# q and k stored as stacked rows, maxima passed through DRAM: a decoder layer in float32 on one core

## The chip, the cores and the metric

The kernel runs on one core of a Trainium2 chip. The metric is the device time of one execution in microseconds, median of three runs. Engines are named as in the profile: PE (TensorE matmul) and PEld (its weight load), DVE (VectorE), ACT (ScalarE), POOL (GpSimd), SP (SyncE). SP computes nothing: it issues nearly all DMAs and waits on semaphores between them.

## The reference

Input x is [8, 256, 256] in float32, 2048 tokens of width 256. Three blocks are applied in turn, each to a layer norm of x and added to x:

1. a gated state-space mixer (projections, a depthwise convolution, a cumulative product and sum along the sequence);
2. attention. The reference passes the normed x as queries and a second tensor as keys and values: `q = Q @ WQ + bQ`, `k = K @ WK + bK`, `v = V @ WV + bV`, 16 heads of 16 columns each, `scores = q k^T / 4` with a causal mask over 256 x 256, a softmax, the product with v, and `@ WO + bO`;
3. a mixture of 8 experts, the top 2 of each token with a capacity per expert.

## The kernel before

The program has two functions that run one after the other with a barrier between their blocks.

**The first, mixer_and_projections**, runs the mixer over four blocks of 512 tokens and computes q, k and v. q and k are kept in two float32r parts, high and low (the low part is the value less its high part), in the tiles `qkh` and `qkl` of [128 features, 2, 512 tokens]. The same two tiles serve k of one block and q of another in turn, so ACT's `k_high` and `q_high` wait until the stores of the other have landed. `store` (L265) writes each part to its own DRAM tensor, `qd[0]`, `qd[1]`, `kd[0]`, `kd[1]`, with one DMA of 128 partitions each. Before the block ends SP waits for all stores.

**The second, attention_route_experts**, goes over 16 groups g. A group is one sequence b of 256 tokens and one half k of the heads (8 heads: 4 pairs, the two heads of a pair at partitions 0 and 64). Each group has three steps s, so there are 48 steps. A step of a group does, by engine:

- PE `scores(u)` (L1363): a first product of q and k, used only for the row maxima of the softmax. DVE `maxima(u)` (L1574) reduces it to one number per query and head.
- PE `turn_maxima(g)` (L1424), once in a group: turns the maxima of the three steps into rows. ACT `maxima_high` and DVE `maxima_low` (L1578) split them into two parts in the tile `mt` of [8 heads, 2 parts, 256].
- SP `maxima(g)` (L1091): copies these rows into the tile `q3` of the group, under the rows of q, one DMA of 1 KB per head and part (16 DMAs a group).
- PE `turned(n)` (L1389): the product again, the other way round, over 50 rows: 16 rows of q high, 16 of q high, 16 of q low against k high, k low, k high (a product in two parts each), and two rows of maxima against rows of -1, so that the maximum is subtracted in the product. It waits for `m_in`, the landing of the maxima.
- ACT `exps(n)` (L1243), PE `weigh(n)` (L1411) against v and against ones, DVE `divide(g)` (L1583, L1586).

The order of each engine is written out by hand, over a step counter t. PE runs `scores(t + LEAD)` beside `turned(t)`, with LEAD = 6, `turn_maxima(g)` in step t = 3g - 3 and `weigh(t - 1)`; masks are added to each product first (L1350, L1375), which wait for DVE's maxima and for ACT's exponentials of the step before, since each product has one PSUM buffer of two banks. Routing of a block of 512 tokens is strewn in between at fixed offsets in the steps: PROJECT, BOTH, NORM, TURN, LOGITS (DVE `choose`, L1610 to L1632), RANKS (`place`, L1638 to L1646) and SEND (POOL `scatter`, L1173). After the last step come the rest of the routing and the experts, which PE bounds (L101, L1516).

SP's list in this function is: `lay(0)`, `lay(1)`, values and small weights, `lay(2)`, `values(1)`, the first expert's weights (two DMAs of 1 MB), `lay(3)`, and then for each g: `lay(g + 2)`, `maxima(g)`, sometimes `values` and `store_base`. `lay(g)` (L1082) fills `q3` and `k3` of a group, 48 rows for each of the two heads of a pair, with 12 DMAs of 64 KB onto 16 partitions each; there are 4 such pairs of tiles (ITEMS), and `lay(g)` waits until `turned` of group g - 4 is done. The first `lay` waits for eight memsets of POOL (L1204) that write the rows of -1.

Of the kernel before, what the change touches and what calls it, by code (L numbers as in the profile page):

```python
# [14 lines left out]
P = 128  # L15
# [153 lines left out]
def mixer_and_projections(nc, sems, c, x_sb, bo, a, disp, qd, kd, vd):  # L169

    with ExitStack() as ctx:
# [69 lines left out]
        with nc.Block() as block:  # L241

            @block.sync
            def _(sp):
# [64 lines left out]
                sp.wait_ge(S["q_st"], 32 * NBLK)  # L309
                sp.wait_ge(S["k_st"], 32 * NBLK)  # L310
# [73 lines left out]
            def _(act):  # L384
# [93 lines left out]
                def k_high(i):  # L478
                    if i == 0:
                        act.wait_ge(S["in_rest"], 80)  # L480
                    for m in range(DC):
                        act.wait_ge(S["k"], DC * i + m + 1)
                        ge(act, S["k_st"], 32 * i)
                        ge(act, S["q_st"], 32 * (i - 1))
# [8 lines left out]
                def q_high(i):  # L493
                    for m in range(DC):
                        act.wait_ge(S["q"], DC * i + m + 1)
                        act.wait_ge(S["k_st"], 32 * upto(i + 2))
                        ge(act, S["q_st"], 32 * i)
# [487 lines left out]
def attention_route_experts(nc, sems, c, x_sb, bo, wo_w, router_w, qd, kd, vd, disp, w1, w2, out):  # L985
# [9 lines left out]
    LEAD = 6  # L995
    ITEMS = 4
    LAID = 16 * 12
    PROJECT, BOTH, NORM, TURN, LOGITS, RANKS, SEND = 8, 14, 16, 17, 20, 23, 24
    END = 12 * (NBLK - 1) + SEND + TPB * K

    with ExitStack() as ctx:
# [68 lines left out]
        with nc.Block(no_gpsimd_drain=True) as block:  # L1070

            @block.sync
            def _(sp):
                def lay(g):
                    b, k = divmod(g, 2)
                    ge(sp, A["st"], 3 * (g - ITEMS + 1))
                    for m, srcs in ((q3[g % ITEMS], (qd[0], qd[0], qd[1])), (k3[g % ITEMS], (kd[0], kd[1], kd[0]))):
                        for n, src in enumerate(srcs):
                            heads = src[k * P:(k + 1) * P, b * L:(b + 1) * L].rearrange("(p e r) t -> e r p t", p=4, e=2)
                            for e in range(2):  # L1080
                                at = 64 * e + HD * n
# [51 lines left out]
                for g in range(GR):  # L1133
# [105 lines left out]
            def _(act):  # L1239
# [5 lines left out]
                def maxima_high(g):  # L1245
                    act.wait_ge(A["mT"], g + 1)
                    ge(act, A[f"m_in{g % 2}"], 256 * (g // 2))
# [51 lines left out]
                maxima_high(0)  # L1299
                for t in range(END):  # L1300
                    if t < NS:
                        exps(t)
                    if t % 3 == 0 and t // 3 + 1 < GR:
                        maxima_high(t // 3 + 1)
# [32 lines left out]
            def _(pe):  # L1337
# [40 lines left out]
                def turned(n):  # L1378
                    g, s = divmod(n, 3)
                    if s == 0:  # L1380
                        pe.wait_ge(A[f"m_in{g % 2}"], 256 * (g // 2 + 1))
# [34 lines left out]
                def turn_maxima(g):  # L1416
                    pe.wait_ge(A["nm"], 3 * g + 3)
                    ge(pe, A["ml"], g)
                    i = (3 * g - 3 - LOGITS) // 12
                    ge(pe, R["i8"], TPB * (i + 1))  # L1420
                    i = (3 * g - 3 - RANKS) // 12
# [33 lines left out]
                def logits(i):  # L1455
                    pe.wait_ge(S["xt"], 2 * (i + 1))
                    pe.wait_ge(A["ml"], min(4 * i + 8, GR))
# [8 lines left out]
                def ranks(i):  # L1466
                    pe.wait_ge(R["both"], i + 1)
                    pe.wait_ge(A["ml"], min(4 * i + 9, GR))
# [321 lines left out]
```

## Time and profile before

| | |
|---|---|
| median of 3 runs | 905.03 us (902.49 to 905.58) |
| the profiled execution's own time | 904.72 us |
| its span, first to last instruction | 903.0 us |
| first function, up to the stores' landing | 0 to about 271 us |
| attention: head, up to the first `turned` | about 271 to 320 us |
| attention: `turned` of 16 groups | 320 to 572 us |
| rest of the routing | 572 to 616 us |
| experts and their output | 616 to 903 us |
| PE busy | 678.1 us (75%) |
| DVE, ACT, POOL busy | 56%, 38%, 36% |

The busy shares are means over stages with different limits. The chain that ended last is followed back from the last instruction; "SPq" in it is time in which SP's queue was issuing DMAs one after another.

### The profile page before, as it was taken

To read this page: it belongs to the slowest core of one execution; us is meant where nothing else is said; L and a number is where in the kernel's file an instruction comes from. 1 tells how busy PE (TensorE), PEld (TensorE's weight loads), DVE (VectorE), ACT (ScalarE), POOL (GpSimd) and SP (SyncE) were. 2 spreads that over 40 slices of the span, in tenths; PEclk is the share of its full clock that TensorE was granted. 3 is DMA by queue.
4 is the path that set the end of the run, shared out by engine and by line. 5 is a ranking of instruction groups with operands and counts; after the bars stand their busy time and mean duration, and the time that the engine had idled before them with its cause. 6 is when DMAs were issued, how large, how long until landed. Compare 5 with 4: busy or idle time off the path is not lost.

```text
span 903.0 us, 13776 instructions
## 1 busy us (share of the span) xinstructions
PE 678.1 (75%) x4984; PEld 561.2 (62%) x4984; DVE 508.2 (56%) x985; ACT 346.5 (38%) x674; POOL 325.3 (36%) x307
## 2 busy tenths in 40 slices
PE   3869989798642357667667857733999999999992
PEld 2548877687431134344344535423999999999992
DVE  6686877869431224444544533422678777787741
ACT  4555647244310022223223213112556556565541
POOL 1326232423007000001113013052457776866855
PEclk9889999999875566879977878755999999999997
DMA  9002056211213632222323311115043454351213
GB/s 293 16 25 94 24 189 211 97 48 52 88 46 95 198 109 57 60 75 57 92 53 112 89 50 58 31 32 186 1 130 62 107 144 96 75 144 17 31 20 40
DMA packets 65987, 76.81 MB, mean 85 GB/s; under 512 B 17739, under 2 KB 52566, under 8 KB 65920
## 3 DMA queue, kind: packets, MB, share of 16 engines
q1 hardware_dynamic: 56704, 68.12, 23.8%
q0 software_dynamic: 9216, 7.81, 6.1%
q8 instruction: 40, 0.66, 0.3%
q14 instruction: 27, 0.22, 0.1%
HBM read 47.75 MB, written 29.64 MB: 86 GB/s over the span
## 4 chain that ended last, share of the span: by engine, by line
SPq 28%; PE 28%; issue 6%; POOL 4%; DMA 2%; DVE 1%; ACT 1%; POOLq 0%
SPq L1091 17%; PE w_bank L1516 13%; PE w_bank L101 11%; SPq L1082 10%; POOL out L1197 2%; PE w_bank L1485 1%; DMA a_q<-a_mt 1%; POOL a_k L1204 1%; POOL disp L1173 1%; POOL w_hl L1186 1%; DMA w_rows<-disp 1%; PE a_turned L1389 0%; DMA out<-w_y,w_to 0%; PE a_out L1411 0%; PE a_shared L1462 0%
## 5 line engine op out<-in xcount | busy, mean ns | idle before, releaser
L1574 DVE TENSOR_REDUCE a_nm<-a_scores 128x4 f32<-128x1024 f32 (+1 forms) x48 | 58.6, 1221 | 158.4 <-PE a_scores L1363 158.4
L1243 ACT ACTIVATE a_pr<-a_turned 128x1024 f32<-128x1024 f32 x48 | 49.2, 1025 | 197.5 <-PE a_turned L1389 197.5
L1516 PE MATMUL w_bank<-w_w2h,w_hh 128*108 128x256 f32 x384 | 108.6, 283 | 1.3 <-POOL w_hl L1186 1.3
L1516 PE MATMUL w_bank<-w_w2h,w_hl 128*108 128x256 f32 x384 | 107.8, 281 | 0.0
L1516 PE MATMUL w_bank<-w_w2l,w_hh 128*108 128x256 f32 x384 | 107.5, 280 | 0.0
L1677 DVE SCALAR_TENSOR_TENSOR w_v<-w_th,w_bank 128x324 f32<-128x324 f32 x128 | 62.8, 492 | 70.2 <-ACT w_th L1281 68.4
L1180 POOL TENSOR_TENSOR w_w1l<-w_s,w_w1h 128x256 fp32r<-128x256 f32 x64 | 56.7, 886 | 120.1 <-ACT w_w1h L1270 120.1
L1281 ACT ACTIVATE w_th<-w_bank 128x324 f32<-128x324 f32 x128 | 56.6, 443 | 99.8 <-PE w_bank L101 98.0
L1389 PE MATMUL a_turned<-a_q,a_k 50*128 50x256 f32 (+1 forms) x256 | 33.2, 364 | 81.9 <-DMA a_q<-a_mt 81.9
L1186 POOL TENSOR_TENSOR w_hl<-w_v,w_hh 128x324 fp32r<-128x324 f32 x64 | 56.5, 882 | 91.4 <-ACT w_hh L1287 91.4
L1389 PEld LDWEIGHTS a_turned<-a_q,a_k 50*128 50x128 f32 x256 | 22.3, 228 | 99.4 <-DMA a_q<-a_mt 90.2
L101 PE MATMUL w_bank<-w_xh,w_w1h 128*128 128x324 f32 x256 | 80.5, 315 | 1.1 <-ACT w_xh L1276 1.1
L101 PE MATMUL w_bank<-w_xh,w_w1l 128*128 128x324 f32 x256 | 80.1, 313 | 0.0
L1197 POOL DMA_INDIRECT out<-w_y,w_to x48 | 75.4, 1570 | 13.2 <-issue 9.9
L101 PE MATMUL w_bank<-w_xl,w_w1h 128*128 128x324 f32 x256 | 80.1, 313 | 0.0
L1653 DVE TENSOR_TENSOR w_w2l<-w_s,w_w2h 128x256 fp32r<-128x256 f32 x64 | 66.2, 1035 | 2.2
L1516 PEld LDWEIGHTS w_bank<-w_w2h,w_hh 128*108 128x108 f32 x384 | 65.8, 171 | 1.8 <-issue 1.8
L1516 PEld LDWEIGHTS w_bank<-w_w2l,w_hh 128*108 128x108 f32 x384 | 66.0, 172 | 0.0
L1516 PEld LDWEIGHTS w_bank<-w_w2h,w_hl 128*108 128x108 f32 x384 | 65.9, 172 | 0.0
L1287 ACT ACTIVATE w_hh<-w_v 128x324 fp32r<-128x324 f32 x128 | 60.3, 472 | 12.0 <-DVE w_v L1677 11.0
L101 PE MATMUL m_bank<-m_sh,m_wh 128*128 128x512 f32 x112 | 46.6, 416 | 10.3 <-ACT m_sh L422 6.9
L1173 POOL DMA_INDIRECT disp<-w_x,w_si x32 | 31.7, 990 | 58.8 <-DVE w_si L1646 46.3
(211 smaller groups left out, 1686.3 us busy)
## 6 DMA issues: line engine op xcount, KB each, us to landing
w_s<-in_L_ffn_w SPq DMA_DIRECT2D x16, 1024.0 KB, 5.0
a_q<-qd SPq DMA_DIRECT2D x96, 64.0 KB, 3.2
a_k<-kd SPq DMA_DIRECT2D x96, 64.0 KB, 2.3
disp<-c_blank SPq DMA_DIRECT2D x8, 658.1 KB
w_rows<-disp SPq DMA_DIRECT2D x8, 658.1 KB
vd<-m_vf SPq DMA_DIRECT2D x4, 1024.0 KB, 4.5
a_v<-vd SPq DMA_DIRECT2D x8, 512.0 KB, 4.2
a_q<-a_mt SPq DMA_DIRECT2D x256, 1.0 KB
```

The costliest lines, as they stand in the source:

```text
L101: mm = pe.matmul(out, a, b, start=first and n == 0, stop=last and n == 3 * len(parts) - 1)
L1082: sp.dma_start(m[at:at + HD, :, :].bitcast(F32), heads[e])\
L1091: sp.dma_start(q3[g % ITEMS][at:at + 1, p, :].bitcast(F32), mt[g % 2][h:h + 1, n, :].bitcast(F32))\
L1180: pool.tensor_tensor(w1_piece(w1l, f), w1_piece(s1[e % 2], f), w1_piece(w1h, f).bitcast(F32), ALU.subtract)\
L1186: pool.tensor_tensor(hl[:, g % 3, half(1)], v[:, n % 4, :], hh[:, g % 3, half(1)].bitcast(F32), ALU.subtract)\
L1197: pool.indirect_dma_start(out=out, out_offset=bass.IndirectOffsetOnAxis(ap=to[:, e % 3, t:t + 1], axis=0), in_=y[e % 2][:, t, :], in_offse ...
L1281: act.activation(th[:, n % 2, :], hb[n % 3][:, 0:HALF], ACT.Tanh, scale=0.5).then_inc(F["th"], 1)
L1287: act.activation(hh[:, g % 3, half(u)], v[:, n % 4, :], ACT.Copy).then_inc(F["hh"], 1)
L1516: mm = pe.matmul(eb[t // 2][0:SP_, (t % 2) * D:(t % 2 + 1) * D], a[:, g % 3, s], w2_piece(b, f), start=f == 0 and t % 2 == 0 and n == 0, s ...
L1574: dve.tensor_reduce(dst, src, AX.X, ALU.max).then_inc(A["nm"], 1)
L1653: dve.tensor_tensor(w2_piece(w2l, f), w2_piece(s2[e % 2], f), w2_piece(w2h, f).bitcast(F32), ALU.subtract)\
L1677: dve.scalar_tensor_tensor(v[:, n % 4, :], th[:, n % 2, :], 1.0, hb[n % 3][:, 0:HALF], ALU.add, ALU.mult).then_inc(F["v"], 1)
```

## The change

- q and k are each one DRAM tensor of 768 rows. The columns of WQ, WK and their biases are permuted on the host (`by_pair`) so that the feature order is half, head of a pair, row within a head, pair. `store` writes six DMAs of 64 partitions (256 KB each) instead of two of 128 partitions (512 KB each): the high part twice and the low part once, in the order in which the rows are stacked in `q3` and `k3`. The semaphores count 96 a store instead of 32.
- `lay(g)` issues four DMAs of 48 partitions (192 KB each) instead of twelve.
- `maxima(g)` writes `mt` to a DRAM tensor `md` with one DMA, waits for it, and reads it back into `q3` with two DMAs. `maxima_high` waits for the write of `md` two groups before rather than for the landing.
- LEAD is 7. `turn_maxima(g)`, `maxima_high` and `maxima_low` move from step 3g - 3 to step 3g - 4, the two of groups 0 and 1 ahead of step 0. LOGITS, RANKS and SEND are one step later.
- SP's `values` and `store_base` move to even g.

The core of the diff (the changed counts of the semaphore waits are left out):

```diff
                 def store(i, dst, sem, done):
                     sp.wait_ge(S[done], DC * (i + 1))
-                    for m, part in enumerate((qkh, qkl)):
-                        sp.dma_start(dst[m][:, i * BLK:(i + 1) * BLK].rearrange("(k p) t -> p k t", p=P),
-                                     part[:, :, :].bitcast(F32)).then_inc(S[sem], 16)
+                    for e in range(2):
+                        for n, part in enumerate((qkh, qkh, qkl) if dst is qd else (qkh, qkl, qkh)):
+                            sp.dma_start(dst.rearrange("(k e s q) n -> e s q k n", k=DC, e=2, s=3)[e, n][:, :, i * BLK:(i + 1) * BLK],
+                                         part[64 * e:64 * e + 64, :, :].bitcast(F32)).then_inc(S[sem], 16)
...
-    LEAD = 6
+    LEAD = 7
-    LAID = 16 * 12
-    PROJECT, BOTH, NORM, TURN, LOGITS, RANKS, SEND = 8, 14, 16, 17, 20, 23, 24
+    LAID = 16 * 4
+    PROJECT, BOTH, NORM, TURN, LOGITS, RANKS, SEND = 8, 14, 16, 17, 21, 24, 25
...
-                    for m, srcs in ((q3[g % ITEMS], (qd[0], qd[0], qd[1])), (k3[g % ITEMS], (kd[0], kd[1], kd[0]))):
-                        for n, src in enumerate(srcs):
-                            heads = src[k * P:(k + 1) * P, b * L:(b + 1) * L].rearrange("(p e r) t -> e r p t", p=4, e=2)
-                            for e in range(2):
-                                at = 64 * e + HD * n
-                                sp.dma_start(m[at:at + HD, :, :].bitcast(F32), heads[e])\
-                                    .then_inc(A[f"laid{g % ITEMS}"], 16)
+                    for m, src in ((q3[g % ITEMS], qd), (k3[g % ITEMS], kd)):
+                        rows = src.rearrange("(k e s r p) n -> k e (s r) p n", k=DC, e=2, s=3, r=HD)
+                        for e in range(2):
+                            sp.dma_start(m[64 * e:64 * e + 3 * HD, :, :].bitcast(F32), rows[k, e][:, :, b * L:(b + 1) * L])\
+                                .then_inc(A[f"laid{g % ITEMS}"], 16)
 
                 def maxima(g):
                     sp.wait_ge(A["ml"], g + 1)
-                    for n in range(2):
-                        for e in range(2):
-                            for p in range(4):
-                                at, h = 64 * e + 3 * HD + n, 4 * e + p
-                                sp.dma_start(q3[g % ITEMS][at:at + 1, p, :].bitcast(F32), mt[g % 2][h:h + 1, n, :].bitcast(F32))\
-                                    .then_inc(A[f"m_in{g % 2}"], 16)
+                    sp.dma_start(md.rearrange("(g n h) t -> g h n t", n=2, h=8)[g], mt[g % 2][:, :, :].bitcast(F32)).then_inc(A["md"], 16)
+                    sp.wait_ge(A["md"], 16 * (g + 1))
+                    for e in range(2):
+                        at = 64 * e + 3 * HD
+                        sp.dma_start(q3[g % ITEMS][at:at + 2, :, :].bitcast(F32),
+                                     md.rearrange("(g n e p) t -> g e n p t", n=2, e=2, p=4)[g, e]).then_inc(A[f"m_in{g % 2}"], 16)
...
-                    if g % 2 == 1 and 3 <= g and (g - 3) // 2 + 2 < B:
-                        values((g - 3) // 2 + 2)
-                    if g % 4 == 3 and g >= 7:
-                        store_base((g - 7) // 4)
+                    if g % 2 == 0 and g >= 4:
+                        values(g // 2)
+                    if g % 4 == 0 and g >= 8:
+                        store_base(g // 4 - 2)
+                store_base(NBLK - 2)
                 store_base(NBLK - 1)
...
-                    if t % 3 == 0 and 0 <= t // 3 + 1 < GR:
-                        turn_maxima(t // 3 + 1)
+                    if t % 3 == 2 and 0 <= (t + 4) // 3 < GR:
+                        turn_maxima((t + 4) // 3)
```

## Rows read from the trace of the kernel before

**Rows 1.** Busy time by stage: head, steps of attention, experts.

```profile
core 0: us, PE busy (x) PEld busy (x) DVE busy (x) ACT busy (x) POOL busy (x), PEclk, DMA share, GB/s
279.00:320.00 41.00, 11.05 (x50) 5.15 (x50) 7.76 (x7) 0.37 (x1) 9.51 (x7) 0.50 0.54 161
320.00:572.00 252.00, 175.37 (x1768) 112.60 (x1768) 112.83 (x219) 63.69 (x89) 31.96 (x30) 0.79 0.27 73
616.00:903.00 287.00, 262.40 (x2016) 260.92 (x2016) 188.33 (x376) 149.88 (x376) 180.86 (x168) 0.96 0.36 82
```

**Rows 2.** The page's chain that ended last, by line.

```profile
SPq L1091 17%; PE w_bank L1516 13%; PE w_bank L101 11%; SPq L1082 10%; POOL out L1197 2%; PE w_bank L1485 1%; DMA a_q<-a_mt 1%; POOL a_k L1204 1%; POOL disp L1173 1%; POOL w_hl L1186 1%; DMA w_rows<-disp 1%; PE a_turned L1389 0%; DMA out<-w_y,w_to 0%; PE a_out L1411 0%; PE a_shared L1462 0%
```

**Rows 3.** Waits, 324 to 545 us: us in total, times, longest.

```profile
PE a_turned L1389 <- DMA a_q<-a_mt: 61.2, 13, 8.2
PEld a_scores L1350 <- DVE a_nm L1574: 6.8, 13, 2.4
```

**Rows 4.** SP's timeline, one round (start us, us, what).

```profile
454.25 2.92 SPq L1082 DMA_DIRECT2D a_q<-qd  x6
461.09 9.98 SPq L1091 DMA_DIRECT2D a_q<-a_mt  x16
...
471.74 2.84 SPq L1082 DMA_DIRECT2D a_q<-qd  x6
```

**Rows 5.** PE's timeline: turned waiting for maxima: first and last of 16.

```profile
320.45 0.80 PE L1389 MATMUL a_turned<-a_q,a_k 50*128 50x256 f32 x4 [16.68 <-DMA a_q<-a_mt]
...
571.53 0.80 PE L1389 MATMUL a_turned<-a_q,a_k 50*128 50x256 f32 x4 [2.40 <-DMA a_q<-a_mt]
```

**Rows 6.** The page's costliest groups: all 16 waits of turned together.

```profile
L1389 PE MATMUL a_turned<-a_q,a_k 50*128 50x256 f32 (+1 forms) x256 | 33.2, 364 | 81.9 <-DMA a_q<-a_mt 81.9
```

**Rows 7.** Short stretches (columns as in Rows 1): store, lay, large loads.

```profile
268.00:270.00 2.00, 0.00 (x0) 0.00 (x0) 0.00 (x0) 0.00 (x0) 0.00 (x0) 0.50 0.99 371
281.00:285.00 4.00, 0.00 (x0) 0.00 (x0) 0.00 (x0) 0.00 (x0) 4.00 (x3) 0.50 0.44 137
303.00:306.00 3.00, 0.77 (x2) 0.00 (x0) 0.00 (x0) 0.00 (x0) 0.00 (x0) 0.50 1.04 415
```

**Rows 8.** SP's timeline: last store, first lay, larger loads.

```profile
266.69 0.47 SPq L265 DMA_DIRECT2D qd<-m_qkl  x1
278.81 2.68 SPq L1082 DMA_DIRECT2D a_q<-qd  x6
...
301.15 0.47 SPq L1101 DMA_DIRECT2D w_s<-in_L_ffn_w  x1
```

**Rows 9.** PE's timeline in the head: first scores, last masks of scores.

```profile
286.25 1.12 PE L1363 MATMUL a_scores<-a_k,a_q 48*128 48x128 f32 x8 [14.35 <-DMA a_k<-kd]
...
302.74 1.03 PE L1350 MATMUL a_scores<-c_mask,c_identb 128*128 128x512 bf16 x2 [0.79 <-DVE a_nm L1574]
```

**Rows 10.** The chain of waits around the first maxima (start us, us, what).

```profile
318.71 1.70 DMA a_q<-a_mt
...
322.00 0.96 PE a_shared L1424 x4
323.83 0.50 SPq L1091
```

**Rows 11.** DVE's timeline: choose of one block, divide and split, the maxima behind.

```profile
433.87 0.37 DVE L1610 MAX8 w_m<-a_shared 128x8 f32<-128x8 f32 x4
...
436.23 0.17 DVE L1632 TENSOR_TENSOR w_x<-w_wr,w_x 128x4 f32<-128x4 f32 x1
...
439.81 1.76 DVE L1583 RECIPROCAL a_rc<-a_out 128x256 f32<-128x256 f32 x1 [0.92 <-PE a_out L1411]
...
442.60 1.22 DVE L1574 TENSOR_REDUCE a_nm<-a_scores 128x4 f32<-128x1024 f32 x1
```

**Rows 12.** SP's store of the tiles, and ACT's next write of them.

```profile
222.15 0.47 SPq L265 DMA_DIRECT2D kd<-m_qkl  x1
231.70 0.69 ACT L498 ACTIVATE m_qkh<-m_bank,m_bq 128x512 fp32r<-128x512 f32 x1 [5.24 <-PE m_bank L101]
```

More of the change, by code:

```diff
@@ L308, in _ @@
                                          c["blank"][:, :, :]).then_inc(S["blanked"], 16)
-                sp.wait_ge(S["q_st"], 32 * NBLK)
-                sp.wait_ge(S["k_st"], 32 * NBLK)
+                sp.wait_ge(S["q_st"], 96 * NBLK)
+                sp.wait_ge(S["k_st"], 96 * NBLK)
                 sp.wait_ge(S["v_st"], 16 * NBLK)
@@ L482, in k_high @@
                         act.wait_ge(S["k"], DC * i + m + 1)
-                        ge(act, S["k_st"], 32 * i)
-                        ge(act, S["q_st"], 32 * (i - 1))
+                        ge(act, S["k_st"], 96 * i)
+                        ge(act, S["q_st"], 96 * (i - 1))
                         act.activation(qkh[:, m, :], pair(i, "K", m)[:, :], ACT.Identity, bias=bk[:, m:m + 1]).then_inc(S["kh"], 1)
@@ L495, in q_high @@
                         act.wait_ge(S["q"], DC * i + m + 1)
-                        act.wait_ge(S["k_st"], 32 * upto(i + 2))
-                        ge(act, S["q_st"], 32 * i)
+                        act.wait_ge(S["k_st"], 96 * upto(i + 2))
+                        ge(act, S["q_st"], 96 * i)
                         act.activation(qkh[:, m, :], pair(i + 2, "Q", m)[:, :], ACT.Identity, bias=bq[:, m:m + 1]).then_inc(S["qh"], 1)
@@ L1299, in _ @@
                 maxima_high(0)
+                maxima_high(1)
                 for t in range(END):
@@ L1302, in _ @@
                         exps(t)
-                    if t % 3 == 0 and t // 3 + 1 < GR:
-                        maxima_high(t // 3 + 1)
+                    if t % 3 == 2 and (t + 4) // 3 < GR:
+                        maxima_high((t + 4) // 3)
                     if due(t, NORM) is not None:
@@ L1418, in turn_maxima @@
                     ge(pe, A["ml"], g)
-                    i = (3 * g - 3 - LOGITS) // 12
+                    i = (3 * g - 4 - LOGITS) // 12
                     ge(pe, R["i8"], TPB * (i + 1))
-                    i = (3 * g - 3 - RANKS) // 12
+                    i = (3 * g - 4 - RANKS) // 12
                     ge(pe, R["tmp"], i + 1)
@@ L1456, in logits @@
                     pe.wait_ge(S["xt"], 2 * (i + 1))
-                    pe.wait_ge(A["ml"], min(4 * i + 8, GR))
+                    pe.wait_ge(A["ml"], min(4 * i + 9, GR))
                     ge(pe, R["i8"], TPB * i)
@@ L1467, in ranks @@
                     pe.wait_ge(R["both"], i + 1)
-                    pe.wait_ge(A["ml"], min(4 * i + 9, GR))
+                    pe.wait_ge(A["ml"], min(4 * i + 10, GR))
                     ge(pe, R["tmp"], i)
@@ L1695, in _ @@
                         maxima(u)
-                    if t % 3 == 0 and 0 <= t // 3 + 1 < GR:
-                        maxima_low(t // 3 + 1)
+                    if t % 3 == 2 and 0 <= (t + 4) // 3 < GR:
+                        maxima_low((t + 4) // 3)
                     if t % 3 == 0 and 1 <= t // 3 <= GR:
@@ L1741, in build @@
         disp = nc.dram_tensor("disp", (E * SLOTS, XW), F32).ap()
-        qd = [nc.dram_tensor(f"qd{n}", (D, N), F32).ap() for n in range(2)]
-        kd = [nc.dram_tensor(f"kd{n}", (D, N), F32).ap() for n in range(2)]
+        qd = nc.dram_tensor("qd", (3 * D, N), F32).ap()
+        kd = nc.dram_tensor("kd", (3 * D, N), F32).ap()
+        md = nc.dram_tensor("md", (2 * B * K * 8, L), F32).ap()
         vd = nc.dram_tensor("vd", (N, HEADS * VP), F32).ap()
@@ L1747, in build, with by_pair @@
         mixer_and_projections(nc, sems, c, x_sb, bo, a, disp, qd, kd, vd)
-        attention_route_experts(nc, sems, c, x_sb, bo, a["L0_xattn_WO"], a["L0_ffn_router_w"], qd, kd, vd, disp,
+        attention_route_experts(nc, sems, c, x_sb, bo, a["L0_xattn_WO"], a["L0_ffn_router_w"], qd, kd, vd, md, disp,
                                 a["L0_ffn_w1"], a["L0_ffn_w2"], out)
+def by_pair(v):
+    return v.reshape(DC, 4, 2, HD, -1).transpose(0, 2, 3, 1, 4).reshape(v.shape)
 def layout(inputs):
@@ L1758, in layout @@
         short = name.replace("L0_attn_", "")
+        if name in ("L0_xattn_WQ", "L0_xattn_WK", "L0_xattn_bQ", "L0_xattn_bK"):
+            v = by_pair(v.T).T
         if name.startswith("L0_attn_") and short in MIX or name == "L0_ffn_router_w":
```

6 lines of the change are left out of this document (3 added, 3 removed).

## The prediction, made before the changed kernel was seen to run

> **What bounds the kernel now.** I read the busy time by stage first, since the means over the span mix stages with different limits. In the experts PE is busy for 262 of 287 us; the diff touches nothing there. Over the steps of attention PE is busy for 175 of 252 us, DVE for 113, ACT for 64, at a granted clock of 0.79: nobody is the bound by his own work [rows 1]. The chain that ended last names who is: SP's queue at the maxima (L1091, 17% of the span) and at the loads (L1082, 10%), some 250 us together [rows 2]. SP's timeline shows the same as a beat. A round of loads begins at 454.25 and the next at 471.74, 17.5 us later, and nearly all of it is issuing: 12 loads of some 0.5 us and 16 maxima in 9.98 us, 0.62 each [rows 4]. SP waits for nobody; everybody waits for SP. On PE this shows as one wait a group, of `turned` for the maxima: 16 waits, 81.9 us [rows 6], the first of them 16.68 us [rows 5]. Other waits are small beside it: PE's mask waits for DVE's maxima for 6.8 us in 13 groups where the maxima's DMAs cost 61.2 [rows 3].
>
> So between the first `turned` (320.45) and the sixteenth (571.53) lie 251.1 us, of which 81.9 - 16.7 = 65.2 are waits for SP, and 185.9 us, 12.4 a group, are PE with its small waits [rows 5, 6].
>
> **The change part by part.** The sum is made against the profiled execution's own 904.7 us, 0.3 below the median.
>
> *SP's round.* Its price lies in the number of DMAs, not their bytes: a load of 64 KB takes 0.45 us to issue (2.68 for six), one of 1 MB 0.47 [rows 8]. Twelve loads become four, 5.5 to 1.9 us; sixteen maxima become three issues, 10.0 to 1.6 us. What comes in is the wait for the write of `md`, behind which the read of the maxima and then the next `lay` are queued on SP. A small transfer landed 1.70 us after its last issue [rows 10]. So a round is 1.9 + 1.6 + some 2 = 5.5 us, up to 8 if `md`'s write lies behind the loads in the DMA engines. Both are far below 12.4: SP ceases to be the bound.
>
> *Do the maxima arrive in time?* In the new order `turned(3g - 4)` lets SP issue `lay(g + 2)`, the same step turns the maxima, and `turned(3g)` needs them four steps later. Before, SP could start the maxima 3.4 us after a `turned` began (320.45 to 323.83), at half clock [rows 5, 10]. From there: 0.5 issue and 1.7 landing; that write may lie behind 786 KB of loads, which at 371 GB/s take 2.1 us and at the 137 GB/s of the small loads 5.7 [rows 7]; then 1.1 for two issues and 1.7 landing. That is 8.4 us, with the loads ahead 10.5 to 14. Four steps of a 12.4 us group are 16.5, and 14.7 were a group as short as 11. It fits; the wait of `turned` goes to zero or nearly so. The loads themselves have three steps, some 12 us, for 1.9 + 2.1 + 2: they fit too. The late one next is then PE itself.
>
> *PE, DVE and ACT without SP's wait.* Two terms of opposite sign. The clock: granted 0.79 in the steps, 0.96 where PE is fed [rows 1]. All 175 us of PE work at 0.79 taken to 0.96, with nothing else to hold it, would give -31, and no change of clock 0. I take -7, nearer to the second: the steps keep small gaps, and much of PE's time in a step is its start on another engine's result. Against it: DVE's side work lay in the wait for SP. `choose` takes 2.5 us (433.87 to 436.40), and after the move it stands in the step of `divide` (1.76 + 0.42), in front of the maxima of the next step (`divide` and the split of w2 already hold them from 439.81 to 442.60) [rows 11]. A step has some 4 us, so the mask would wait 2 to 3 us for each block, some 1 us for each projection: 4 us in four groups, +7 over the stage. Bounds 0 and +25 (every microsecond of `choose`, projection and norm laid open). Net 0, from -15 to +15 for both together.
>
> *The head.* Before: stores landed at about 270.85, eight memsets, `lay(0)` at 278.81 [rows 8], scores from 286.25, the masks of the seventh scores at 302.74 [rows 9], then 16.7 us of waiting for 48 loads and 16 maxima in SP's queue. After: (a) the last store has 1.57 MB instead of 1.05 and six issues. At 371 GB/s [rows 7] this is +1.4 us, at 137, which is what DMAs onto 16 partitions moved while SP paced them, +8.6. A store of 64 partitions is nearer to the first; +2.4. (b) PE's own chain: it was ready for `turned` at 303.8, the end of the masks at 302.74; one scores more (2.75 us, a sixth of 286.25 to 302.74) [rows 9]; `lay(0)` complete some 2.3 us earlier for its shorter issue: 303.8 + 2.4 + 2.75 - 2.3 = 306.7. (c) The transfers: ahead of `md`'s write lie 6.5 MB (four lays 3.15, values 1.05, expert weights 2.1, WO 0.26). At 371 GB/s 17.6 us, from 281.2 plus 2 for the first landing and 4.5 for writing and reading the maxima: 305.3; at 137 for the lays and 415 for the rest 319. I take 307.5 for the first `turned`, 13 us earlier than 320.45; from 305 to 319.
>
> *Costed at nothing.* The stores within the first function: the closest reuse has ACT write the tiles at 231.70 after a store issued until 222.62 [rows 12]. The new store needs 1.6 us more of issue and 1.4 more of transfer upon the 4.2 from 266.7 to 270.9, 7 to 8 us of these 9; if that cover is gone, some 2 us. The permutation is the host's. `values` and `store_base` are one issue each, behind the maxima and needed a group later; uncovered, 0.5 us a time. LOGITS, RANKS and SEND a step later: after the last step the steps hold nothing, so the end of the routing starts from the same work.
>
> **Sum:** 904.7 - 13 (head) - 65.2 (waits of 15 groups) + 0 = 826.5.
>
> **A rule against the change.** The row of the first loads, onto 16 partitions each, has the DMA engines busy 0.44 of the time for 137 GB/s, or 311 at full share; 128 partitions give 371 to 415 at a share near 1 [rows 7]. The trace thus shows no halving, but it has no transfer of 48 or 64 partitions. The Trainium skill, page SBUF — State Buffer, section on the DMA port swizzle, says that a transfer over partitions 0 to 63 reaches only half of the 16 ports, and that two such transfers, one to each half, serialize; it gives some 218 GB/s. By it the estimate would be that last store and head take together some 6 us more, and the sum would be 833.
>
> **The rivals.**
>
> 1. *Half rate for 48 and 64 partitions.* At half of 371, 186 GB/s, the last store takes +5.6, the lays of the head 17 instead of 8.5 us: the first `turned` at 281.2 + 3.2 + 2 + 17 + 9 + 4.5 = 317. The maxima's path grows to some 12.5 us, still inside 14.7 to 16.5. Time 904.7 - 3.5 - 65.2 = 836, and if some groups wait 1 us, 842. For it: there is no row of such a transfer, and the slowest rows are those with the fewest partitions; against it: the share of 0.44. 0.15.
> 2. *DVE and ACT become the bound of the steps.* The side work is laid open by +15 rather than +7, with no gain of clock: 841. For it: DVE's 113 us are 0.61 of the 186 that remain, and it has one buffer of scores; against: only 6.8 us of such waits now. 0.17.
> 3. *The clock gives more.* The steps at 0.96 and DVE's work in the gaps: -12, 814. 0.12.
> 4. *Issue goes by descriptors,* so the change doesn't save what it says: a load of 192 KB at three times 0.45 us makes `lay` 5.4 again. SP's round is then 9 us, still under 12.4, but the maxima's path 12 to 17: some groups wait 2 us, 850. Against: 0.47 us for 1 MB. 0.03.
> 5. *The round trip takes SP's place.* `md`'s write, its wait and the read behind 786 KB of loads, once a group, on a path of four steps. It decides from 14 us on; the group is then three quarters of the path, and slower than now from 17.3 / 0.75 = 23 us on, where my path has 10.5. At 25 us a group takes 18.75, 15 groups 281 us instead of 251: 904.7 - 13 + 30 = 922. It needs loads at some 50 GB/s; the slowest row has 137, paced by SP. 0.03.
>
> **How the numbers follow.** My forecast, between 818 and 834, has 0.50. With rivals 1 to 3 the span from 812 to 846 holds a bit over 8 in 10, so that is the range. A measurement of this kernel tells about 0.3%, 2.7 us, from no change: every case but the last lies far beyond it. Faster 0.96, same 0.01, slower 0.03.
>
> **What would show it.** SP's timeline: rounds of 4 + 1 + 2 DMAs with idle time between them. PE: `turned` waits for the maxima only in the first group, near 307; then about 185 us to the sixteenth. Granted clock in the steps near 0.9. Waits of the masks for DVE's maxima up from 7 us to 15 or so. DMA rate of the last store: 370 or 190. I am wrong if `turned` still waits each group (rivals 1, 4, 5), if the group is 13.4 (rival 2), or if SP's issue of `lay` is above 3 us.

## The result and the profile after

The changed kernel takes 828.31 us (median of 4 runs, 822.04 to 831.38) against 905.31 us (902.49 to 906.53): a ratio of 0.9145, interval 0.9083 to 0.9206. I had said 826.5, from 812 to 846. Its profiled execution is the fastest of the four, 822.04 us, with a span of 820.3; the others are 4 to 9 us longer, at a mean granted clock of 0.881 to 0.887 against its 0.888. So trace against trace the change is -82.7 us, median against median -77.0.

The page's chain that ended last, by engine. SP's queue stood in it with 27% of the span [rows 2]; now with 2%:

```profile
PE 42%; DVE 9%; issue 5%; POOL 4%; DMA 3%; SPq 2%; ACT 1%; POOLq 0%; ACTq 0%
```

Busy time of the changed kernel by stage, as in [rows 1]: head, steps, experts; below them two stretches of the last store and one of the first loads, as in [rows 7]:

```profile
core 0: us, PE busy (x) PEld busy (x) DVE busy (x) ACT busy (x) POOL busy (x), PEclk, DMA share, GB/s
281.00:310.00 29.00, 13.49 (x64) 6.57 (x64) 9.40 (x9) 0.74 (x2) 10.45 (x9) 0.50 0.89 227
310.00:488.00 178.00, 153.44 (x1758) 96.75 (x1760) 107.00 (x196) 62.43 (x87) 31.88 (x30) 0.91 0.39 107
...
533.00:820.00 287.00, 263.39 (x2016) 261.92 (x2016) 188.43 (x376) 149.90 (x376) 180.84 (x168) 0.95 0.36 82
...
266.00:268.00 2.00, 0.00 (x0) 0.00 (x0) 0.00 (x0) 0.00 (x0) 0.00 (x0) 0.50 1.01 200
268.00:270.00 2.00, 0.00 (x0) 0.00 (x0) 0.00 (x0) 0.00 (x0) 0.00 (x0) 0.50 0.98 216
284.00:287.00 3.00, 0.00 (x0) 0.00 (x0) 0.00 (x0) 0.00 (x0) 3.00 (x3) 0.50 0.99 216
```

The steps shrank from 252 to 178 us and PE's own work in them from 175 to 153 us, at a granted clock of 0.91 instead of 0.79 (a mean of stretches at the two levels, 1.2 and 2.4 GHz). The experts didn't move. Transfers of 64 and 48 partitions move 200 to 216 GB/s in these stretches with the DMA engines fully busy, where 128 partitions had 371.

SP's timeline (start us, us, what): the last store, the head, and one round in the steps, which answers to [rows 4] and [rows 8]:

```profile
264.31 1.23 SPq L266 DMA_DIRECT2D qd<-m_qkh  x2
...
268.90 1.19 SPq L266 DMA_DIRECT2D qd<-m_qkl  x1
281.81 1.25 SPq L1081 DMA_DIRECT2D a_q<-qd  x2
...
296.10 3.34 SPq L1081 DMA_DIRECT2D a_q<-qd  x2
...
300.77 0.50 SPq L1086 DMA_DIRECT2D md<-a_mt  x1
308.64 0.56 SPq L1090 DMA_DIRECT2D a_q<-md  x2
...
409.11 1.19 SPq L1081 DMA_DIRECT2D a_q<-qd  x2
410.35 1.25 SPq L1081 DMA_DIRECT2D a_k<-kd  x2
411.64 0.49 SPq L1086 DMA_DIRECT2D md<-a_mt  x1
415.70 0.53 SPq L1090 DMA_DIRECT2D a_q<-md  x2
416.29 0.38 SPq L1095 DMA_DIRECT2D a_v<-vd  x1
422.56 1.20 SPq L1081 DMA_DIRECT2D a_q<-qd  x2
```

The round of 17.5 us is gone: four loads in 2.5 us, the maxima's three issues in 1, between them 3.6 us of waiting for the write of `md`, and then SP has nothing to do until 422.56.

PE's timeline, for [rows 9] and [rows 5]: first scores, first `turned`, one wait for the exponentials, `turned` of the sixteenth group:

```profile
288.18 1.12 PE L1364 MATMUL a_scores<-a_k,a_q 48*128 48x128 f32 x8 [13.28 <-DMA a_k<-kd]
...
310.53 0.80 PE L1390 MATMUL a_turned<-a_q,a_k 50*128 50x256 f32 x4 [1.84 <-DMA a_q<-md]
...
392.32 0.61 PE L1376 MATMUL a_turned<-c_identb,c_mask 128*128 128x512 bf16 x2 [2.27 <-ACT a_pr L1243]
...
487.53 0.50 PE L1390 MATMUL a_turned<-a_q,a_k 50*128 50x256 f32 x4
```

And the waits from 300 to 500 us, as in [rows 3] (us in total, times, longest):

```profile
PEld a_scores L1351 <- DVE a_nm L1575: 18.3, 21, 2.4
...
PEld a_turned L1376 <- ACT a_pr L1243: 13.5, 20, 3.1
PE a_scores L1351 <- DVE a_nm L1575: 11.4, 10, 1.9
ACT w_ex L1265 <- DVE w_d L1616: 10.6, 3, 3.7
PE a_turned L1376 <- ACT a_pr L1243: 7.9, 4, 2.6
...
PE a_turned L1390 <- DMA a_q<-md: 1.8, 1, 1.8
```

This window takes in the end of the head. Over the steps alone (310.5 to 487.6 us) the first of these rows is 14.8 us; before it was 7.1 (320.4 to 571.6 us).

`turned` waited 16 times, 81.9 us [rows 6]; it now waits once, 1.8 us. What PE waits for instead is DVE (the maxima of the scores, behind its side work) and ACT (the exponentials).

The stages add up: first `turned` at 310.53 instead of 320.45, -9.9; from the first to the sixteenth 177.0 instead of 251.1, -74.1; from there to the end 820.3 - 487.53 = 332.8 instead of 903.0 - 571.53 = 331.5, +1.3. Sum -82.7.

### The profile page after: what moved, and what is told of

It reads as the page before. It is cut to its first block, busy times and chain, and to the rows that moved or that the text cites. A ratio compares the mean times of both kernels' runs of the same rounds, so it can differ in the third digit from the quotient of the medians.

```text
span 820.3 us, 13471 instructions
## 1 busy us (share of the span) xinstructions
PE 658.7 (80%) x4984; PEld 547.7 (67%) x4984; DVE 506.4 (62%) x985; ACT 345.7 (42%) x674; POOL 325.1 (40%) x307
## 4 chain that ended last, share of the span: by engine, by line
PE 42%; DVE 9%; issue 5%; POOL 4%; DMA 3%; SPq 2%; ACT 1%; POOLq 0%; ACTq 0%
PE w_bank L1517 14%; PE w_bank L101 13%; DVE a_nm L1575 3%; DVE a_rc L1584 3%; PE a_out L1412 2%; PE a_turned L1390 2%; POOL out L1197 2%; PE a_shared L1440 2%; SPq L1081 1%; PE a_turned L1376 1%; PE a_scores L1351 1%; PE w_bank L1486 1%; PE a_scores L1364 1%; PE a_shared L1463 1%; DMA md<-a_mt 1%
## 5 line engine op out<-in xcount | busy, mean ns | idle before, releaser
L1197 POOL DMA_INDIRECT out<-w_y,w_to x48 | 75.3, 1570 | 13.2 <-issue 9.9
L101 PEld LDWEIGHTS w_bank<-w_xh,w_w1h 128*128 128x128 f32 x256 | 49.0, 192 | 1.4 <-ACT w_xh L1276 1.4
L101 PEld LDWEIGHTS w_bank<-w_xl,w_w1h 128*128 128x128 f32 x256 | 49.2, 192 | 0.0
```

The lines of the kernel that those rows point to most:

```text
L101: mm = pe.matmul(out, a, b, start=first and n == 0, stop=last and n == 3 * len(parts) - 1)
L1197: pool.indirect_dma_start(out=out, out_offset=bass.IndirectOffsetOnAxis(ap=to[:, e % 3, t:t + 1], axis=0), in_=y[e % 2][:, t, :], in_offse ...
```

## The experiments

My theory was that the three parts pay through SP's queue alone, nearly all of it through the maxima, and that the steps are now held by the order of side work on DVE and ACT, the head by stores, memsets and loads. Rivals: that the restacked loads or the seventh step carry the gain. "Steps" below is the time from the first to the sixteenth `turned`; before it is 251.1, changed 177.0. All kernels compute everything that the changed kernel does.

### Which part carries the gain

**Maxima by row.** The sixteen small DMAs back, with the semaphore counts and the wait of `maxima_high` that go with them; all else as changed.

```diff
-    sp.dma_start(md..., mt[g % 2]...); sp.wait_ge(A["md"], 16 * (g + 1))
-    for e in range(2):
-        sp.dma_start(q3[g % ITEMS][at:at + 2, :, :]..., md...[g, e])
+    for n in range(2):
+        for e in range(2):
+            for p in range(4):
+                sp.dma_start(q3[g % ITEMS][at:at + 1, p, :]..., mt[g % 2][h:h + 1, n, :]...)
```

> The changed kernel with one part undone: the maxima go straight into q3 with 16 DMAs of 1 KB, no DRAM and no wait on SP. Theory, SP's count of issues is the price: a round of SP is 2.5 us of loads and 10.1 of maxima, with values and stores some 13 us, above the 11.8 a group takes now. So turned waits for the maxima in most groups again, a group takes 13.1, and the time is near 850 us (845 to 860). Rival, the round trip through DRAM costs about what the sixteen issues did, and only the loads mattered: 828 or a little less, with no waits of turned.

Measured: 854.26 us (852.69 to 860.36), ratio 0.9461, interval 0.9415 to 0.9507; steps 209.5. SP's timeline in it, and its waits from 300 to 500 us:

```profile
408.12 10.07 SPq L1090 DMA_DIRECT2D a_q<-a_mt  x16
```

```profile
PEld a_turned L1390 <- DMA a_q<-a_mt: 25.6, 10, 5.1
PE a_turned L1390 <- DMA a_q<-a_mt: 22.5, 10, 4.8
```

With four loads but sixteen maxima SP's round is 2.5 + 10.1 and whatever else it issues, and `turned` waits in ten of the groups again. The steps are 32.5 us longer than in the changed kernel: 19.1 us are waits of `turned` behind its first, and 13.2 are PE's own work, 166.6 us instead of 153.4, at a clock of 0.84 instead of 0.91. The maxima in three issues are worth 26 us on top of the rest, 33.6 trace against trace. The same run shows the other side: four loads and the seventh step without the new maxima already take 49 us off the kernel before (903.59 to 854.26).

**Twelve loads.** The storage, the stores of 128 partitions and the twelve loads of before; maxima through DRAM and seven steps as changed.

```diff
-    LAID = 16 * 4
+    LAID = 16 * 12
...
-    for m, src in ((q3[g % ITEMS], qd), (k3[g % ITEMS], kd)):
+    for m, srcs in ((q3[g % ITEMS], (qd[0], qd[0], qd[1])), ...):
```

> The changed kernel with the other part undone: the two DRAM tensors of before, stores of 128 partitions, twelve loads a group; maxima through DRAM and seven steps kept. Theory of the count of issues: a round is 5.5 of loads, 1.5 of maxima and 3 to 3.5 us of waiting for md, some 10.5 to 11.5, just under a group; the steps stay near 11.8 a group. The last store lands 3 us earlier, the head's SP queue is 11 us longer but its transfers are faster, first turned near 313. Time 832 us (826 to 842). Rival, both parts were needed to bring SP under PE: turned waits in most groups, 845 to 860.

Measured: 827.49 us (824.62 to 834.22), ratio 0.9178, interval 0.9137 to 0.9219: as fast as the changed kernel. Its steps take 176.6 us. Its head in three timelines: POOL's first memset, SP's last store, first load and first maxima, PE's first `turned`:

```profile
268.73 7.93 POOL L1205 MEMSET a_k<- 32x1024 f32 x8 [14.88 <-POOLq L241]
```

```profile
264.15 0.36 SPq L265 DMA_DIRECT2D qd<-m_qkh  x1
...
276.69 2.69 SPq L1082 DMA_DIRECT2D a_q<-qd  x6
...
307.21 0.33 SPq L1087 DMA_DIRECT2D md<-a_mt  x1
```

```profile
314.09 0.80 PE L1391 MATMUL a_turned<-a_q,a_k 50*128 50x256 f32 x4 [9.66 <-DMA a_q<-md]
```

POOL's first memset in the changed kernel, and in the kernel before:

```profile
273.85 7.93 POOL L1204 MEMSET a_k<- 32x1024 f32 x8 [19.85 <-POOLq L241]
```

```profile
270.85 7.93 POOL L1204 MEMSET a_k<- 32x1024 f32 x8 [14.82 <-POOLq L241]
```

From the first issue of the last store to the memset it needs 4.6 us, the changed kernel 9.5 (264.31 to 273.85): the restacked storage costs 5.0 us there. Its 48 loads then cost more issue, and `turned` is 3.6 us later than in the changed kernel. One round of SP in its steps:

```profile
400.31 2.68 SPq L1082 DMA_DIRECT2D a_q<-qd  x6
...
406.95 0.33 SPq L1087 DMA_DIRECT2D md<-a_mt  x1
408.75 0.54 SPq L1091 DMA_DIRECT2D a_q<-md  x2
```

That is 9.0 us (400.31 to 409.29) against 7.1 in the changed kernel (409.11 to 416.23), both less than the 11.8 of a group. Four loads save 4.1 us of issue in this round, but 2.3 of them come back as a longer wait for `md`, 4.1 us from its issue instead of 1.8. So here the restacking brings nothing that the runs can tell. The two runs together say that either cut, with the seventh step, takes most of the gain by itself, the loads 49 us and the maxima 76 of the 77: what counts is SP's round against PE's group, and the cut of the maxima is enough to bring it under.

**Six steps.** LEAD back to 6, `turn_maxima` and the routing at their steps of before; loads and maxima as changed.

```diff
-    LEAD = 7
-    PROJECT, BOTH, NORM, TURN, LOGITS, RANKS, SEND = 8, 14, 16, 17, 21, 24, 25
+    LEAD = 6
+    PROJECT, BOTH, NORM, TURN, LOGITS, RANKS, SEND = 8, 14, 16, 17, 20, 23, 24
...
-                    if t % 3 == 2 and (t + 4) // 3 < GR:
-                        maxima_high((t + 4) // 3)
+                    if t % 3 == 0 and t // 3 + 1 < GR:
+                        maxima_high(t // 3 + 1)
```

> The changed kernel with LEAD back at 6 and the maxima turned in step 3g - 3, LOGITS, RANKS and SEND as before. Theory: from turned to the landing of the maxima the path is some 7 us when md is not behind the loads, three steps are 11.8, so nothing waits and the time is that of the changed kernel, 828 us (822 to 833); choose leaves the step of divide, worth up to 2 us. Rival, the round trip needs the seventh step: turned waits 2 to 4 us in each group, 860 to 885.

Measured: 822.77 us (818.52 to 827.14), ratio 0.9094, interval 0.9047 to 0.914; steps 179.6. `turned` waits for the maxima once, 6.01 us in the first group, and never after. The fourth step of lead isn't needed with four loads; three hold the round trip. With twelve loads no run has six steps. From the sixteenth `turned` to the end it takes 329.5 us, 3.3 less than the changed kernel, where LOGITS and RANKS stand a step later; but that stretch takes 331.5 us in the kernel before, with LOGITS at the same step as here, so the step of the routing alone doesn't explain it.

### The head

**Memsets by tile.** The first loads of q wait for no memset; each load of k waits for its own two.

```diff
-                sp.wait_ge(A["minus"], 2 * ITEMS)
                 lay(0)
...
+                        if m is k3[g % ITEMS] and g < ITEMS:
+                            sp.wait_ge(A["minus"], 2 * (g + 1))
```

> The changed kernel, but SP no longer waits for all eight memsets of the rows of -1 ahead of its first load: the loads of q3 go at once, those of each k3 wait for the two memsets of that tile. Theory, the head is the sum of SP's start, the transfers and the steps of scores: first load 8 us earlier, first scores 5.5 us earlier, first turned near 304 instead of 310.5, time 6 us less than the changed kernel, 822. Rival, the head is bound by its 6.5 MB of transfers at half rate or by POOL: 828, first turned near 309.

Measured: 816.96 us (815.92 to 817.49), ratio 0.9035, interval 0.9018 to 0.9052. The first load goes out at 276.15 instead of 281.81, the first `turned` runs at 306.06, 4.5 us earlier, still after a wait of 1.84 for the maxima. In this execution the last store was first issued 2.3 us later (266.61), so counted from there the first load is 8.0 us earlier, as expected, and the first `turned` 6.8. The profiled execution is 5.2 us shorter, the median 11.4; the changed kernel's runs spread over 9 us and these over 1.6, and why is open.

**Halves of the store.** Is it the count of 64 partitions, or the order of the two halves? In the kernel before, each store is cut in two by partitions; in the changed kernel the two halves alternate instead of going three and three.

```diff
 (kernel before)
-                        sp.dma_start(dst[m]..., part[:, :, :].bitcast(F32))
+                        for e in range(2):
+                            sp.dma_start(dst[m]...[64 * e:64 * e + 64], part[64 * e:64 * e + 64, :, :].bitcast(F32))
 (changed kernel)
-                    for e in range(2):
-                        for n, part in enumerate(...):
+                    for n, part in enumerate(...):
+                        for e in range(2):
```

> The kernel before with one thing changed: each store of q and k in two DMAs of 64 partitions, the same 1.05 MB to the same places. Theory, half the partitions of a transfer give about half the rate, whatever is stored: the last store moves at 200 to 216 GB/s instead of 371 and lands some 2 us later, time 907 us. Rival, the low rate seen in the changed kernel comes from its three stacked copies or their rows: the rate stays near 371, time 905.

> The changed kernel with the six DMAs of a store in another order: lower and upper half of the partitions by turns instead of three and three. Theory of the Trainium skill (page SBUF - State Buffer, section on two DMAs for both halves): they serialize, so the rate stays near 216 GB/s and the time at 828 us (822 to 831). Rival, transfers to different halves run beside each other once they are neighbours in the queue: the last store moves at 300 GB/s or more and lands 2 to 3 us earlier, 825.

Measured, one execution each: 905.26 us for the first, 820.09 us for the second; single executions can't tell these times from those of the uncut kernels. Stretches of the last store, first in the kernel before with cut stores, then in the changed kernel with halves by turns:

```profile
268.00:270.00 2.00, 0.00 (x0) 0.00 (x0) 0.00 (x0) 0.00 (x0) 0.00 (x0) 0.50 0.93 273
```

```profile
266.00:268.00 2.00, 0.00 (x0) 0.00 (x0) 0.00 (x0) 0.00 (x0) 0.00 (x0) 0.50 0.94 273
268.00:270.00 2.00, 0.00 (x0) 0.00 (x0) 0.00 (x0) 0.00 (x0) 0.00 (x0) 0.50 0.86 267
```

Neither expectation holds: by turns the halves reach 267 to 273 GB/s in these stretches, more than the 200 to 216 in sequence and less than 371. The loop of the first kernel also issues lower and upper half by turns, so both runs test that order, and none has the old storage with its halves in sequence. From the first issue of the last store to the memset the second kernel takes 8.2 us (263.71 to 271.89) instead of 9.5, and the first 6.3 us (265.65 to 271.93) instead of 4.6.

**Head together.** Memsets by tile, halves by turns, and the first expert's weights (2 MB) issued behind the first maxima instead of ahead of `lay(3)`.

```diff
-                weights(0)
                 lay(3)
...
                     if g == 0:
+                        weights(0)
                         weights(1)
```

> The changed kernel with the head alone altered: memset wait by tile (817 us by itself), stores of the two halves by turns, and the first expert's weights issued behind the first maxima. Theory, the last store lands 1.4 us earlier (0.5 to 2), and the write of md no longer lies behind 2 MB, so PE's 1.84 us of waiting goes; beyond that the scores of the head set the pace: 814 us (811 to 817). Rival, the weights now collide with the second group's maxima or hold ACT's exponentials, the gain is given back: 817 to 821.

Measured: 813.03 us (812.06 to 815.0), ratio 0.9024, interval 0.9006 to 0.9042: as expected. The first `turned` runs at 300.45 without a wait. From the first scores on (280.02) it is PE's chain with DVE's maxima between the scores that bounds the head then.

### The order of side work in the steps

**Divide a step later.** DVE's `divide` leaves the step in which `choose` stands.

```diff
-                    if t % 3 == 0 and 1 <= t // 3 <= GR:
+                    if t % 3 == 1 and 1 <= t // 3 <= GR:
                         divide(t // 3 - 1)
```

> The changed kernel with one line moved: DVE's divide of a group runs one step later, behind the maxima of that step instead of ahead of the maxima of the next. The work is the same. Theory, what holds a group at 11.8 us now is the order of DVE's side work (divide, and choose behind it, which also keeps ACT's exponentials waiting), not PE's own work: the masks' waits for maxima and the waits for the exponentials fall by half, the steps from 177 to some 167 us, the time is 818 us. Rival, PE's work and its clock bound the steps: 828, the waits only move elsewhere.

Measured: 838.98 us (837.81 to 842.88), ratio 0.93, interval 0.9271 to 0.9329: 11 us slower than the changed kernel, where I had expected a gain. Its waits from 315 to 490 us, and its PE timeline, first here, then in the changed kernel:

```profile
PE a_shared L1440 <- DVE a_ot L1587: 14.8, 6, 2.5
```

```profile
336.34 3.48 PE L1440 MATMUL a_shared<-w_wo,a_ot 128*128 128x256 f32 x8 [2.53 <-DVE a_ot L1587]
```

```profile
333.49 1.97 PE L1440 MATMUL a_shared<-w_wo,a_ot 128*128 128x256 f32 x8
```

Over the steps PE's waits in the masks did fall, for DVE from 8.8 to 4.1 us and for the exponentials from 5.2 to 1.1. But the output projection (L1440) stands at a fixed step and reads what `divide` writes: now it waits for it, some 2.5 us in each of six, 16.1 us over the steps where the changed kernel has 1.3. The steps take 196.8 us; PE's own work in them is 161.7 us at a clock of 0.86, where the changed kernel has 153.4 at 0.91. The matmuls of the projection shown took 3.48 us at a granted clock of 0.56, the changed kernel's 1.97 at 1.00.

**Both.** Memsets by tile and divide later.

> The changed kernel with the memset wait by tile and divide one step later together. Theory, they lie in different stretches (head, steps) and add: 817 less what divide alone gives, near 807. Rival, they overlap or divide does nothing: 815 to 817.

Measured: 831.2 us (827.07 to 833.09), ratio 0.9184, interval 0.9155 to 0.9213: 7.8 below the divide alone (4.7 trace against trace, where the memsets by tile gave 5.2). The two add within what the runs can tell; the expectation fell with the one before.

**Projection later too.** If the lost cover of the projection is the whole of that miss, moving the consumer as well must turn it round. This edit also moves `choose` and the other routing, and the waits for the maxima that go with LOGITS and RANKS.

```diff
-    PROJECT, BOTH, NORM, TURN, LOGITS, RANKS, SEND = 8, 14, 16, 17, 21, 24, 25
+    PROJECT, BOTH, NORM, TURN, LOGITS, RANKS, SEND = 9, 15, 17, 18, 24, 27, 27
...
-                    if t % 3 == 0 and 1 <= t // 3 <= GR:
+                    if t % 3 == 1 and 1 <= t // 3 <= GR:
```

> The changed kernel with divide one step later, as in the run that was 10 us slower, and the routing behind it moved too: PROJECT, BOTH, NORM, TURN one step later, LOGITS and RANKS three, SEND two, so that choose stands in a step without divide. Theory, in that run the masks' and exponentials' waits did fall, by 20 us, and projection's wait for divide (2.4 us for each of seven sequences) with the slower clock behind it took more than that: with projection a step later both gains stay, the steps go from 177 to about 165 us, time 816 us (810 to 821). Rival, PE's own work bounds the steps and every such wait only moves: 826 to 830.

Measured: 804.29 us (801.58 to 805.13), ratio 0.8923, interval 0.8906 to 0.894. Its steps:

```profile
311.00:469.00 158.00, 144.52 (x1736) 91.06 (x1736) 104.16 (x194) 62.48 (x87) 31.88 (x30) 0.94 0.43 121
```

157.8 us, 10.5 a group: 19 less than in the changed kernel and 39 less than with the divide alone. Better than expected by 12. In the steps the projection no longer waits for `divide`. Of the 19 us, 8.9 are PE's own work (144.5 instead of 153.4, at a clock of 0.94) and 10.3 its idle time. The 20 us of fallen waits in my expectation came from windows of unequal reach; on PE over the steps they were 8.8. How much of the gain is the projection's and how much that of `choose` in another step, this run doesn't separate.

### All together, and the loads once more

**All.** Projection later and the head together.

> Both of the above together: the altered head and the moved divide, projection and choose. Theory, they lie in different stretches and add: 814 less the 12 us of the steps, 802 us (797 to 810). If the steps gained nothing, 814.

Measured: 790.72 us (789.25 to 792.81, 5 runs), ratio 0.8769, interval 0.8751 to 0.8787: the best version, 37.6 us below the changed kernel, 31.1 trace against trace. It lies below my range, since I had counted 12 us for the steps, and they gave 24. The two gains as measured apart, 15.3 and 24.0, add up to 789.0: they do add.

**All, with twelve loads.** The same with the storage, stores and loads of before.

> The fastest variant (head altered, divide, projection and choose moved, 790.7 us) with the storage of q and k of before: two tensors, stores of 128 partitions, twelve loads a group, no permutation. Its groups take 10.4 us instead of 11.8, so SP has less room. Theory, SP's round is 5.5 to 6.7 of loads, some 2.3 for the maxima with their wait and 0.4 for values, about 9 us, still under 10.4: the steps stay at 156 us, the last store lands 2 to 3 us earlier, SP's longer queue in the head takes 3 to 6 back: 792 us (788 to 796). Rival, at this pace the four loads are needed: turned waits in most groups for 1 us or more, 800 to 815.

Measured: 802.95 us (802.48 to 805.22, 5 runs), ratio 0.889, interval 0.8867 to 0.8912. I had expected no difference; it is 12 us (14.3 trace against trace), so restacking with its stores does pay here. The time lies in my rival's range, but not by its mechanism, a wait in most groups: `turned` waits in the first two. `turned` of the first groups on PE, first with four loads, then with twelve:

```profile
302.05 0.79 PE L1391 MATMUL a_turned<-a_q,a_k 50*128 50x256 f32 x4
...
312.72 0.50 PE L1391 MATMUL a_turned<-a_q,a_k 50*128 50x256 f32 x4 [0.55 <-DMA a_q<-md]
...
320.74 0.50 PE L1391 MATMUL a_turned<-a_q,a_k 50*128 50x256 f32 x4
```

```profile
305.21 0.80 PE L1392 MATMUL a_turned<-a_q,a_k 50*128 50x256 f32 x4 [5.01 <-DMA a_q<-md]
...
318.90 0.79 PE L1392 MATMUL a_turned<-a_q,a_k 50*128 50x256 f32 x4 [3.33 <-DMA a_q<-md]
...
329.68 0.50 PE L1392 MATMUL a_turned<-a_q,a_k 50*128 50x256 f32 x4
```

3.2 us are lost before the first `turned` and 5.8 in the next two groups (24.5 us instead of 18.7), where SP is behind with the issues of the head and PE runs on at the lower clock: 0.79 us for a `turned` of 0.50 (318.90 and 312.72), a granted clock of 0.73 over these two groups against 0.84. SP's timeline with twelve loads shows both sides:

```profile
266.86 0.36 SPq L265 DMA_DIRECT2D qd<-m_qkh  x1
...
271.43 3.65 SPq L1084 DMA_DIRECT2D a_q<-qd  x6
...
300.32 0.33 SPq L1089 DMA_DIRECT2D md<-a_mt  x1
```

The first load is out 3.3 us earlier than with four loads (274.76, for the stores of 128 partitions are faster: 4.6 us from first issue to memset against 8.2), and the first maxima are written 7.0 us later than there (293.29). The other 4 us of the steps lie in four single groups, 0.7 to 1.5 us each, and 1.3 us behind the sixteenth `turned`; their cause is open.

## Why the prediction was right, point by point

- **SP's round** (5.5, up to 8): four loads take 2.5 us, not 1.9, for a load of 192 KB costs 0.60 us of issue where I took some 0.47; the maxima's issues take 1.0, not 1.6; the wait for `md` is 3.6 rather than 2. Together some 7 us of 11.8. That SP ceases to be the bound is shown: by the idle time in its queue and by the kernel with maxima by row, in which only SP's issue was put back and the waits came back with it. Rival 4 (issue goes by descriptors) would have made it 1.35 us a load; it fell.
- **The waits of 15 groups, -65.2:** gone, as predicted.
- **The head, -13:** -9.9, so 3.1 short, in four pieces. (a) The memsets began 3.0 us later than before (273.85, 270.85), where I took 2.4. (b) The first scores came 6.4 us after the first load instead of 7.4 (288.18 - 281.81; 286.25 - 278.81), a gain of 1.1 where I took 2.3, the first loads moving at 216 GB/s; the scores themselves took 3.0 us more, where I took 2.75. (c) PE then waited 1.84 us for the maxima behind the transfers, where I had put the first `turned` 0.8 behind PE's own chain; for the transfers I gave 305.3 to 319, and 281:310 ran at 227 GB/s.
- **Term (a) is worse than the trace shows:** counted from the first issue of the last store, the comparison with twelve loads gives +5.0, by the rate of 200 to 216 GB/s; the 5.6 of rival 1 was nearly right. Only 3.0 shows, since the first function happened to end 2 us earlier (264.31; the kernel before had 266.29, and kernels with the old storage, alike in that function, 264.15 and 266.86).
- **Clock against side work, net 0:** the net was -8.9 (177.0 instead of 185.9 without waits), inside my -15 to +15, but both terms were far too small. PE's work fell by 22 us, from 175.4 to 153.4, where I took 7, for the clock went to 0.91; and the time in which PE did nothing in the steps, without the waits for SP, rose from 10.5 to 23.6 us (185.9 - 175.4; 177.0 - 153.4), 13 where I took 7. The +7 didn't even follow from my own numbers: 4 us in each of four groups would be 16, near the 13 that came. That the sum came out right is in part luck, since the two errors have opposite signs. The clock of 0.91 is what I wrote under "what would show it"; 175 us taken from 0.79 to 0.91 give 152, which is what came, and I should have carried it into the sum. In all, the profiled execution took 822.0 us where the sum says 826.5: +3.1 from the head, -8.9 from the steps and +1.3 behind them.
- **A wait I didn't foresee:** ACT's `ratio` (L1265) waits for `choose` and holds the exponentials behind it, 3.7 us at most; PE's masks of `turned` then wait 2.3 to 2.6 us once in each of three blocks, the third behind the sixteenth group's first `turned`.
- **Costed at nothing.** From the sixteenth `turned` to the end it took 1.3 us more than before. Whether that is the routing a step later isn't shown: with LOGITS at 20 this stretch took 331.5 (before) and 329.5 us (six steps), with 21 it took 332.8, and 328.7 with `divide` later. The stores inside the first function cost nothing visible.
- **Rival 1,** half rate for 48 and 64 partitions, was nearly right about the rate (I took 186 GB/s; it was 200 to 216 at 0.98 to 1.01 of the engines' time) and wrong about the price, 836 to 842: the transfers of the head lay almost wholly beside PE's own scores, and those of the steps in SP's free time. The share of 0.44 at 137 GB/s, from which I had argued for 311, is no sign of room: it belongs to another shape. What the Trainium skill says (SBUF — State Buffer, on the DMA port swizzle), that partitions 0 to 63 tend towards some 218 GB/s, agrees with the 216 here. What the same page of the Trainium skill says under "Can I just issue two DMAs to hit both halves?", which is also where the sentence on serializing in my prediction belongs, is that two such transfers gain only 6%. That doesn't agree: by turns the halves got 267 to 273 GB/s against 200 to 216.
- **Rival 2,** DVE and ACT as the bound, names part of what is left, though it didn't set this time: the order of side work alone was worth 24 us (projection later against the changed kernel; 20.4 trace against trace), with DVE's and ACT's work unchanged.
- **Rivals 3 and 5:** the clock did more than I took but not alone; the round trip never came near deciding, since even six steps hold it. The 17.3 us in rival 5 stands in no row; from [rows 5] a group takes 251.1 / 15 = 16.7 us, which moves its threshold from 23 to 22 us and nothing else.

## What to carry to other kernels

Where a queue that only issues DMAs is the bound, price a change by the number of issues, compare the round with what the next engine needs, and test each part alone. Of the three parts here the sixteen maxima made into three were enough, beside the seventh step that all but one kernel kept. The restacked loads with that step bring 49 us alone, nothing on top of the maxima, and 12 us once the next limits were out of the way. The seventh step brought nothing beside four loads. When such a wait goes, work out anew what the clock gives back on PE's whole work in that stage, and which side work loses its cover. Move side work together with whoever reads it: the same divide one step later was 11 us slower alone and part of a gain of 24 us with its projection.

## What the chip showed that I had not expected

- The DMA engines can be fully busy at 200 to 216 GB/s with transfers of 48 or 64 partitions, at 371 to 380 with 128, and two halves of 64 partitions by turns give 267 to 273. Even in sequence the last store has 256 GB/s from 270 to 271 us, about when its lower half must end and its upper half begin (an estimate: 786 KB at 200 GB/s take 3.9 us, from 265.5 on).
- The issue of a DMA on SP costs 0.47 us for 1 MB onto 128 partitions, 0.60 for 192 KB onto 48 and 0.45 for 64 KB onto 16: it follows neither bytes nor number of partitions.
- From the issue of the write of the 16 KB of maxima to the issue of the read it took 4.1 us right behind 786 KB of loads (411.64 to 415.70), and 7.9 us (300.77 to 308.64) behind what was still queued of the head's loads.
- Kernels whose first function is the same reached its last store up to 2.9 us apart (263.71 and 266.56 us, the halves by turns alone and in the version with all changes), which is as much as some of the head's terms.
